# Gated cross-attention and a top-2 expert layer on one core: ranks behind scores and transposes, five groups for six, shares and values on GpSimd, block tables handed over in two parts

## The chip, the cores and the metric

One Trainium2 chip, one core. The metric is device time in microseconds (us) of one execution, median over the runs; lower is better. Engines: PE (TensorE, its weight loads PEld), DVE (VectorE), ACT (ScalarE), POOL (GpSimd), SP (SyncE, which only issues DMAs here). The engines run their own instruction streams and meet at semaphores.

## What is computed

Eight batches of 256 rows of 256 features. First a gated cross-attention over 120 context rows, then a gated mixture of 8 experts with the two best experts per row.

```
x = x + tanh(g_xattn) * attention(layernorm(x), ctx)      # 16 query heads summed to 4, rope, mean over heads, @ Wo
# ffn of layernorm(x), rows flattened to T = 2048:
probs = softmax(x @ gate_w.T);  w, idx = top_k(probs, 2);  w = w / w.sum()
for e in range(8):                                        # combine[t, e] = w where e was picked
    g, u = split(x @ gate_up[e].T, 2)                     # 1024 each
    acc += combine[:, e] * ((silu(g) * u) @ down[e].T)
x = x + tanh(g_ffn) * acc
```

## The kernel before, in words

The work has two halves. The first goes batch by batch through the attention and picks two experts for each row. The second is a loop over blocks: the 4096 picks are sorted by expert, each expert's list is cut into blocks of 128 rows, and PE runs each block through its expert.

First half. All engines run the same loop `for t in range(B + 1)`, a software pipeline: round t works on scores of batch t+1 (`scores`), transposes the probabilities of batch t (`transpose_probs`), mixes its values (`mix_values`), and finishes batch t-1 (`transpose_o`, `attend`; then on DVE `best_two`, which begins with two MAX8 on the gate logits, and `add_residual`, `normalise_o`). ACT does the exponentials and copies out of PSUM, POOL the reciprocal roots, and in the first rounds both split the first expert's weights into a high and a low part.

The routing is done for groups of batches, `SETS`. With `ENDS[b]` the group that ends with batch b: in round b+1 DVE makes the group's choice (`choose`: eight small steps that give `pick` and `chosen`) and `logit_gap`; in round b+2 PE counts, for each pick, how many came before it on its expert (`ranks`, small bf16 matmuls that need `chosen_ready`), DVE turns the ranks into slots (`ranks_of_picks`, `slots`, with a `value` that carries the token's number) and shares (`share_out`: the weight per expert, written beside the row in `x`), POOL marks with a compare against 0..127 at which place in its block each pick goes (`mark_places`, four per batch, called "hits" below), DVE marks which blocks begin at or before its slot, times the value (`mark_slots`, four per batch); in round b+3 PE multiplies the two (`invert`, four matmuls per batch, each two passes and so x8 in the trace), which writes each token's number at its slot, and DVE adds the result up (`add_places`). The marks live in a ring of `DEPTH` = 3 batches. SP stores a group's rows with shares and norm terms in DRAM (`store_rows`). At the end of the loop stand the last inversion, `find_tokens` (the list `token_at`), and the block tables on DVE: which expert each block has, how many blocks there are, where its index column lies (`bases_ready`), and at which block the pieces of the next expert's weights have to be split (`piece_at`, `piece_code`, then `tables_ready`). Meanwhile PE runs `stay_warm(10)`, matmuls whose result nobody reads.

Second half. POOL gathers the rows of each block (indirect DMA, four in flight) and scatters the results with an add. ACT applies the norm (`stage`), PE transposes the block (`transpose_x`), ACT and DVE split it into two fp32r parts (`x_high`, `x_low`), PE expands it in two halves (`expand`), ACT applies silu (`gate`), DVE multiplies (`product`), PE transposes (`transpose_h`) and contracts (`contract`). The next expert's weights are loaded and split beside it. Step 0 stands ahead of the loops; ACT and PE wait for `tables_ready` ahead of it.

## Time and profile before

| | |
|---|---|
| median of 3 runs | 470.66 us (469.97 to 474.62) |
| profiled execution | 469.98 us |
| its span | 468.2 us |
| mean granted TensorE clock | 0.958 |
| PE busy | 429.1 us, 92% |
| PEld / DVE / ACT / POOL busy | 357.5 / 223.0 / 199.2 / 253.7 us |

The span runs from the first to the last record of the profiler; what lies around it belongs to the execution's time too. Busy time of PE is modelled at its ends. A timeline row has start, length, engine, line, operation, output and inputs, the number of instructions merged in it, and in brackets the engine's idle time before it and what ended it. The number after L is the line in the kernel before.

### The profile page before, as it was taken

Reading aid. Unit: us, or ns where it says so; the run is one execution under the profiler, and the core shown is the slowest. Engines: PE = TensorE matmul, PEld = TensorE weight load, DVE = VectorE, ACT = ScalarE, POOL = GpSimd, SP = SyncE. Lnnn points to the kernel's source line nnn. Section 1 sums busy time; section 2 is a strip of 40 time slices with the busy share of each in tenths; the row PEclk is TensorE's granted clock in tenths of the full one; section 3 lists DMA queues with packets and bytes.
Section 4 is the critical chain, followed back from the end, with each engine's and each line's share of the span. In section 5 each row is a group of like instructions: output and inputs, shape, how many; then the busy total and the mean of one; then the engine's idle time right before and its main releaser. Section 6 shows DMA issues by size and latency. Waiting matters only on the chain.

```text
span 468.2 us, 10992 instructions
## 1 busy us (share of the span) xinstructions
PE 429.1 (92%) x2541; PEld 357.5 (76%) x2542; DVE 223.0 (48%) x625; ACT 199.2 (43%) x388; POOL 253.7 (54%) x255
## 2 busy tenths in 40 slices
PE   7899978885999999999999999999999999999960
PEld 6656555763478888888888888888888888888850
DVE  2465979656633434344434444444434443444330
ACT  2477644400166235634633743364336435523310
POOL 3119646433438634972992794269526954954321
PEclk9999999766999999999999999999999999999985
DMA  8950035612104512461353165116411642111211
GB/s 274 401 210 25 22 100 162 216 46 70 36 12 148 180 24 32 123 205 23 101 174 86 26 199 135 23 23 202 124 34 23 202 120 39 22 25 26 47 25 11
DMA packets 19579, 46.54 MB, mean 99 GB/s; under 512 B 2380, under 2 KB 13716, under 8 KB 16468
## 3 DMA queue, kind: packets, MB, share of 16 engines
q1 hardware_dynamic: 11648, 35.20, 22.1%
q0 software_dynamic: 6720, 9.64, 11.2%
q10 hardware_dynamic: 1188, 1.44, 0.9%
q8 instruction: 9, 0.15, 0.1%
q14 instruction: 14, 0.11, 0.1%
HBM read 37.54 MB, written 9.00 MB: 99 GB/s over the span
## 4 chain that ended last, share of the span: by engine, by line
PE 82%; DVE 8%; DMA 3%; issue 3%; ACT 2%; POOL 1%; POOLq 1%; SPq 0%; DVEq 0%
PE sc L908 20%; PE att L928 20%; PE misc L908 10%; PE qbank L908 10%; PE pT L918 6%; PE sc L734 2%; PE att L822 2%; DMA x<-in_x 2%; PE sc L752 2%; PE att L892 2%; PE att L791 2%; PE misc L776 1%; DVE dn L1121 1%; PE att L716 1%; PE misc L768 1%
## 5 line engine op out<-in xcount | busy, mean ns | idle before, releaser
L928 PE MATMUL att<-dn,hT 128*128 x816 | 115.0, 291 | 0.0
L463 POOL DMA_INDIRECT out<-xT_all,index_out x34 | 54.5, 1604 | 109.7 <-DVE xT_all L1315 101.3
L908 PE MATMUL sc<-gu,xT 128*128 x408 | 103.0, 401 | 0.0
L928 PEld LDWEIGHTS att<-dn,hT 128*128 128x128 f32 x816 | 102.7, 192 | 0.1
L908 PEld LDWEIGHTS sc<-gu,xT 128*128 128x128 f32 x408 | 74.2, 188 | 15.0
L908 PE MATMUL misc<-gu,xT 128*128 x204 | 80.0, 392 | 1.7 <-ACT xT L638 0.9
L908 PE MATMUL qbank<-gu,xT 128*128 x204 | 79.9, 392 | 0.0
L374 POOL TENSOR_TENSOR gu<-wraw,gu 128x2048 f32 x14 | 64.5, 4624 | 10.1 <-ACT gu L556 8.0
L1289 DVE TENSOR_TENSOR xT_all<-xT_all,sc 128x512 f32<-128x512 f32 x34 | 23.4, 687 | 88.3 <-ACT xT_all L645 88.3
L1289 DVE TENSOR_TENSOR xT_all<-xT_all,qbank 128x512 f32<-128x512 f32 x34 | 23.4, 688 | 64.1 <-ACT xT_all L645 64.1
L645 ACT ACTIVATE xT_all<-misc 128x512 f32<-128x512 f32 x34 | 20.3, 598 | 71.7 <-PE qbank L908 71.7
L1293 DVE TENSOR_TENSOR hT<-pT,hT 128x512 fp32r<-128x512 f32 x68 | 46.5, 684 | 2.8 <-issue 2.8
L908 PEld LDWEIGHTS misc<-gu,xT 128*128 128x128 f32 x204 | 38.4, 188 | 9.2 <-issue 2.3
L456 POOL DMA_INDIRECT xT_all<-rows_scratch,index_in x37 | 36.7, 993 | 14.2 <-issue 10.4
L908 PEld LDWEIGHTS qbank<-gu,xT 128*128 128x128 f32 x204 | 38.4, 188 | 7.1
L918 PE MATMUL pT<-const,xT_all 128*128 128x128 f32 x272 | 40.7, 272 | 2.0 <-issue 2.0
L918 PEld LDWEIGHTS pT<-const,xT_all 128*128 128x128 f32 x272 | 33.8, 140 | 10.9 <-issue 2.2
L649 ACT ACTIVATE hT<-pT 128x512 fp32r<-128x512 f32 x68 | 40.3, 592 | 3.5 <-PE pT L918 3.5
L645 ACT ACTIVATE xT_all<-sc 128x512 f32<-128x512 f32 x34 | 20.2, 593 | 47.4 <-PE sc L908 47.4
L556 ACT ACTIVATE gu<-wraw 128x2048 f32 (+1 forms) x16 | 30.7, 1920 | 11.4 <-PE att L928 7.5
L374 POOL TENSOR_TENSOR dn<-wraw,dn 128x2048 f32 x7 | 32.2, 4603 | 0.0
L389 POOL TENSOR_SCALAR vareps<-mv 128x2 f32<-128x2 f32 (+1 forms) x11 | 2.5, 231 | 53.3 <-DVE mv L996 53.2
(152 smaller groups left out, 529.7 us busy)
## 6 DMA issues: line engine op xcount, KB each, us to landing
wraw<-in_gu SPq DMA_DIRECT2D x16, 1024.0 KB, 5.5
wraw<-in_dn SPq DMA_DIRECT2D x8, 1024.0 KB, 5.1
x<-in_x SPq DMA_DIRECT2D x8, 266.0 KB, 11.3
xT_all<-in_xT SPq DMA_DIRECT2D x4, 512.0 KB, 11.3
out<-x SPq DMA_DIRECT2D x8, 256.0 KB, 2.2
rows_scratch<-x SPq DMA_DIRECT2D x2, 532.0 KB, 5.4
rows_scratch<-x SPq DMA_DIRECT2D x4, 266.0 KB, 2.7
xT_all<-rows_scratch,index_in POOLq DMA_INDIRECT x37, 2.9
```

Of the source, the lines that this page charges most:

```text
L374: nc.gpsimd.tensor_tensor(piece_of(where, 1, p), wraw[:, p * PIECE:(p + 1) * PIECE], piece_of(where, 0, p), ALU.subtract).then_inc(w_lo, 1)
L456: nc.gpsimd.indirect_dma_start(out=xg[:, q, :], out_offset=None, in_=rows_d, in_offset=bass.IndirectOffsetOnAxis(ap=index, axis=0)) .then_ ...
L463: nc.gpsimd.indirect_dma_start(out=out_d, out_offset=bass.IndirectOffsetOnAxis(ap=index, axis=0), in_=y[:, r, :], in_offset=None, compute_ ...
L556: nc.scalar.activation(piece_of(where, 0, p), wraw[:, p * PIECE:(p + 1) * PIECE], ACT.Copy).then_inc(w_hi, 1)
L645: nc.scalar.activation(silu[:, hf, :], bank[2 * hf][:, :], ACT.Silu).then_inc(silu_made, 1)
L649: nc.scalar.activation(hT[:, hf, 0, :], bank[4 + hf][:, :], ACT.Copy).then_inc(hT_hi, 1)
L734: nc.tensor.matmul(sc[:, 1, :], ident, const[:, 0:512], start=True, stop=True)
L908: mm = nc.tensor.matmul(bank[2 * hf + n][:, :], xT[:, par, xp, k, :], gu_part(where, wp, k * 2 * I + col, HALF), start=(k == 0 and xp == 0 ...
L918: mm = nc.tensor.transpose(bank[4 + hf][:, j * P:(j + 1) * P], h[:, hf, j * P:(j + 1) * P], ident)
L928: mm = nc.tensor.matmul(bank[6][:, 0:D], hT[:, hf, hp, j * P:(j + 1) * P], dn_part(where, wp, (hf * JH + j) * D, D), start=(hf == 0 and j ...
L1289: V.tensor_tensor(h[:, hf, :], silu[:, hf, :], bank[2 * hf + 1][:, :], ALU.mult).then_inc(h_made, 1)
L1293: V.tensor_tensor(hT[:, hf, 1, :], bank[4 + hf][:, :], hT[:, hf, 0, :], ALU.subtract)\
```

## The change

Five groups instead of six: batches 4 and 5 form one. The ring of marks is four deep; the fourth place of the hits and the running sum lie in another buffer that is free by then. On PE the ranks come behind the second scores, in the last round behind the transposes of batch 7, and batches 4 and 5 are inverted behind the last round. The shares and the values are made by POOL, the value is multiplied into the hits there, and DVE's block marks become one wide compare per batch. The last batch's hits are split, two on POOL and two on DVE. In the last round the choice is put in front of the second moments. On DVE the tables up to the block ends are made ahead of the last sum; the tables are handed over in two parts: PE waits for `experts_ready` alone, and the low part of block 0 (`x_low(0, 0)`) is made between the two parts. POOL gathers block 1 ahead of the other index copies. The filler is four matmuls instead of ten.

```diff
-SETS = ((0, 1), (2, 3), (4,), (5,), (6,), (7,))
+SETS = ((0, 1), (2, 3), (4, 5), (6,), (7,))
-DEPTH = 3
+DEPTH = 4
+BY_POOL = 2
...
+            def share_out(g):
+                a, z = tiles_of(g)
+                n = z - a
+                pool.wait_ge(chosen_ready, g + 1)
+                pool.wait_ge(odds_ready, g + 1)
+                n_step[0] += 1
+                nc.gpsimd.tensor_tensor(wpart[:, 0:n, :, :], pick[:, a:z, :, :],
+                                        odds[:, a:z, :].rearrange("p t (k o) -> p t k o", o=1).broadcast_to([P, n, 2, E]),
+                                        ALU.mult).then_inc(pool_step, 1)
+                pool.wait_ge(pool_step, n_step[0])
+                nc.gpsimd.tensor_tensor(x[:, a:z, D:D + E], wpart[:, 0:n, 0, :], wpart[:, 0:n, 1, :], ALU.add)\
+                  .then_inc(row_ready, 1)
+            def place_values(g):
+                a, z = tiles_of(g)
                 pool.wait_ge(slot_ready, g + 1)
+                nc.gpsimd.tensor_tensor(
+                    value[:, a:z, :], c("token")[:, a:z].rearrange("p (t o) -> p t o", o=1).broadcast_to([P, z - a, 2]),
+                    place[:, a:z, :], ALU.subtract).then_inc(value_ready, 1)
+                pool.wait_ge(value_ready, g + 1)
...
-                    ins = nc.gpsimd.tensor_scalar(at_place[:, b % DEPTH, i, :], c("place"), place[:, t, k:k + 1], None,
-                                                  ALU.is_equal)
+                    ins = nc.gpsimd.tensor_scalar(at_place[b % DEPTH][:, i, :], c("place"), place[:, t, k:k + 1],
+                                                  value[:, t, k:k + 1], ALU.is_equal, ALU.mult)
...
-            mark_places(B - 1)
+            share_out(NS - 1)
+            place_values(NS - 1)
+            mark_places(B - 1, BY_POOL)
...
-            for s in range(1, RING):
+            keep_index(index_in, 1, 1)
+            pool.wait_ge(index_kept, 1)
+            gather(1, 1, index_in[:, 1:2])
+            for s in range(2, RING):
                 keep_index(index_in, s, s)
...
             pe.wait_ge(x2_ready, B)
-            invert(B - 2, B - 2, B - 1)
+            late = SETS[NS - 3][0]
+            for b in SETS[NS - 3]:
+                invert(b, late, B - 1)
             ranks(NS - 1)
-            invert(B - 1, B - 2, B - 1)
+            invert(B - 2, late, B - 1)
+            invert(B - 1, late, B - 1)
...
-            stay_warm(10)
+            stay_warm(4)
             transpose_x(0)
-            pe.wait_ge(tables_ready, 1)
+            pe.wait_ge(experts_ready, 1)
...
-                for i in range(PICKS):
-                    t, k = TB * b + i // 2, i % 2
-                    ins = V.tensor_scalar(upto[:, b % DEPTH, i, :], c("begin"), slot[:, t, k:k + 1], value[:, t, k:k + 1],
-                                          ALU.is_le, ALU.mult)
-                ins.then_inc(upto_ready, 1)
+                V.tensor_tensor(upto[:, b % DEPTH, :, :],
+                                c("begin").rearrange("p (o n) -> p o n", o=1).broadcast_to([P, PICKS, SLOTS + 1]),
+                                slot[:, TB * b:TB * (b + 1), :].rearrange("p t (k o) -> p (t k) o", o=1)
+                                .broadcast_to([P, PICKS, SLOTS + 1]), ALU.is_le).then_inc(upto_ready, 1)
...
-            link(V.tensor_scalar(last_block[:, :], endblk[:, E - 1:E], -1.0, None, ALU.add))
+            V.tensor_scalar(last_block[:, :], endblk[:, E - 1:E], -1.0, None, ALU.add).then_inc(experts_ready, 1)
+            x_low(0, 0)
```

PE, from the transposes of batch 7 in the last round to the first of block 0. First before; `misc<-xT_all,gc` are those transposes, L804 to L814 the ranks, L822 the inversion, L791 attending, L734 the filler.

```order
L814 MATMUL sc<-chosen,before_bf 128x16
L776 MATMUL misc<-xT_all,gc 8x256 x2
L779 MATMUL misc<-const,on 64x128 x2
L822 MATMUL att<-dn 128x137 x4
L791 MATMUL att<-wo,oT 128x264 x2
L822 MATMUL att<-dn 128x137 x4
L804 MATMUL sc<-base_bf,ones_bf 128x24
L806 MATMUL sc<-chosen,ones_bf 128x24 x14
L812 MATMUL sc<-chosen,ones_bf 128x16
L812 MATMUL sc<-chosen,ones_bf 128x8
L814 MATMUL sc<-chosen,before_bf 128x24
L822 MATMUL att<-dn 128x137 x4
```

And the same place in the changed kernel, where L840 to L850 are the ranks, L860 the inversion and L827 attending.

```order
L815 MATMUL misc<-const,on 64x128 x2
L840 MATMUL sc<-base_bf,ones_bf 128x16
L842 MATMUL sc<-chosen,ones_bf 128x16 x12
L848 MATMUL sc<-chosen,ones_bf 128x8
L850 MATMUL sc<-chosen,before_bf 128x16
L827 MATMUL att<-wo,oT 128x264 x2
L860 MATMUL att<-dn 128x137 x8
L840 MATMUL sc<-base_bf,ones_bf 128x24
L842 MATMUL sc<-chosen,ones_bf 128x24 x14
L848 MATMUL sc<-chosen,ones_bf 128x16
L848 MATMUL sc<-chosen,ones_bf 128x8
L850 MATMUL sc<-chosen,before_bf 128x24
```

Behind it follow the inversions of batches 6 and 7 (x4 and x4) and four fillers. The ranks have moved behind the transposes, no inversion stands ahead of attending, and eight matmuls of inversion stand ahead of the last ranks where four stood.

DVE, from the last marks to the end of the tables. Before, L1121 are the block marks, L1142 and L1145 the shares, L1130 and L1134 the last sum and the token list.

```order
L1121 TENSOR_SCALAR dn<-const,slot_f,value 128x137 x4
L1233 COPY ends_f<-sc 128x8
L1236 TENSOR_TENSOR area<-ends_f,const 128x128
L1238 TENSOR_REDUCE nblk<-area 128x8
L1142 TENSOR_TENSOR route<-route,odds 128x32
L1145 TENSOR_TENSOR x<-route 128x2x8
L1130 TENSOR_TENSOR dn<-att,dn 128x137
L1134 SCALAR_TENSOR_TENSOR token_at<-dn,const 128x136
L1242 TENSOR_TENSOR area<-const,nblk 128x64
```

In the changed kernel L1172 and L1176 are the last sum and the list, L1181 is `x_low(0, 0)`, and the piece tables begin at L1296.

```order
L1281 MEMSET skip 128x1
L1172 TENSOR_TENSOR area<-att,area 128x137
L1176 SCALAR_TENSOR_TENSOR token_at<-area,const 128x136
L1283 TENSOR_TENSOR area<-endblk,const 128x352
...
L1291 TENSOR_SCALAR tab<-tabf 128x44
L1292 TENSOR_SCALAR last_block<-endblk 128x1
L1181 TENSOR_TENSOR xT<-att,xT 128x256
L1296 COPY piece_at<-startblk 128x8
L1297 TENSOR_SCALAR piece_at<-nblk 128x8
```

The block ends stand ahead of the last sum now, the shares are gone from DVE, and `x_low(0, 0)`, which waits for ACT, stands between the two parts of the tables; before it was behind them.

## Rows read from the trace of the kernel before

**Rows 1.** Busy time by window; the columns are named in the prediction.

```profile
86.50:97.00 10.50, 8.75 (x57) 6.96 (x57) 6.03 (x31) 1.94 (x5) 3.72 (x8) 0.67 0.49 152
97.00:106.00 9.00, 6.35 (x35) 4.14 (x35) 6.00 (x31) 0.75 (x3) 3.71 (x8) 0.62 0.17 59
...
133.90:468.20 334.30, 318.50 (x1942) 281.14 (x1942) 137.39 (x304) 143.67 (x253) 195.59 (x158) 0.98 0.32 84
```

**Rows 2.** Timeline, 52 to 64 us: POOL's split and hits, a cast, first inversion.

```profile
52.57 5.03 POOL L380 TENSOR_TENSOR dn<-wraw,dn 128x512 fp32r<-128x512 f32 x4
52.60 1.27 DVE L1107 CAST slot_f<-slot_i 128x16 f32<-128x16 int32 x1
...
57.81 4.67 POOL L419 TENSOR_SCALAR dn<-const,slot_f 128x128 f32<-128x128 f32 x8 [0.21 <-POOL dn L380]
...
62.82 2.04 PE L822 MATMUL att<-dn 128*128 128x137 f32 x16
```

**Rows 3.** Timeline, 66 to 106 us: the rounds' marks and the round to 76.40.

```profile
66.69 0.25 DVE L1047 MAX8 top<-att 128x8 f32<-128x8 f32 x2 [2.14 <-PE att L791]
...
70.06 0.23 PE L812 MATMUL sc<-chosen,ones_bf 128*128 128x24 bf16 x3 [1.16 <-DVE chosen L1075]
...
71.33 1.16 DVE L1027 TENSOR_REDUCE negmax<-sc 128x8 f32<-128x960 f32 x1 [0.26 <-DVE route L1095]
...
73.43 4.67 POOL L419 TENSOR_SCALAR dn<-const,slot_f 128x128 f32<-128x128 f32 x8 [0.27 <-DVE slot_f L1107]
...
74.07 2.81 ACT L566 ACTIVATE gu<-sc,shift,rs 128x120 f32<-128x120 f32 x8
74.09 2.39 DVE L1121 TENSOR_SCALAR dn<-const,slot_f,value 128x137 f32<-128x137 f32 x8
...
76.40 0.23 DVE L1047 MAX8 top<-att 128x8 f32<-128x8 f32 x2
...
85.86 0.25 DVE L1047 MAX8 top<-att 128x8 f32<-128x8 f32 x2 [1.68 <-PE att L791]
...
96.46 0.25 DVE L1047 MAX8 top<-att 128x8 f32<-128x8 f32 x2 [2.28 <-PE att L791]
...
105.55 0.25 DVE L1047 MAX8 top<-att 128x8 f32<-128x8 f32 x2 [0.80 <-PE att L791]
```

**Rows 4.** Timeline, 107 to 115 us: the last group's ranks, marks and inversion.

```profile
107.08 1.21 PE L822 MATMUL att<-dn 128*128 128x137 f32 x8 [1.57 <-DVE x L1080]
...
109.71 0.19 DVE L1095 TENSOR_TENSOR route<-route,sc 128x32 f32<-128x32 f32 x1 [0.35 <-PE sc L814]
...
110.63 2.42 POOL L419 TENSOR_SCALAR dn<-const,slot_f 128x128 f32<-128x128 f32 x4 [0.86 <-DVE slot_f L1107]
110.69 1.31 DVE L1121 TENSOR_SCALAR dn<-const,slot_f,value 128x137 f32<-128x137 f32 x4
...
113.10 2.20 PE L822 MATMUL att<-dn 128*128 128x137 f32 x8 [3.43 <-POOL dn L419]
```

**Rows 5.** Timeline, 115 to 134 us: filler, tables, step 0, the loop's first matmul.

```profile
115.09 10.53 PE L734 MATMUL sc<-const 128*128 128x512 f32 x20
...
116.99 0.57 DVE L1250 TENSOR_TENSOR area<-endblk,const 128x352 f32<-128x352 f32 x1
...
120.01 0.60 ACT L631 ACTIVATE xT_all<-xT_all 128x256 f32<-128x256 f32 x1 [10.28 <-DMA xT_all<-rows_scratch,token_at]
...
120.34 0.15 DVE L1259 TENSOR_SCALAR last_block<-endblk 128x1 int32<-128x1 f32 x1
...
125.16 0.21 DVE L1277 TENSOR_TENSOR tab<-tabf 128x44 int32<-128x44 f32 x1
...
126.74 0.49 PE L908 MATMUL misc<-gu,xT 128*128 x1 [0.91 <-ACT xT L638]
...
129.84 1.28 ACT L645 ACT_TABLE_LOAD   x1 [2.43 <-PE qbank L908]
...
133.90 0.49 PE L908 MATMUL misc<-gu,xT 128*128 x1 [0.71 <-issue]
```

More of the change, by code:

```diff
@@ L190, in build_program @@
         hits = dn[:, 1, :, :].rearrange("p q n -> p (q n)").bitcast(F32)
-        at_place = hits[:, 0:DEPTH * PICKS * P].rearrange("p (q i n) -> p q i n", q=DEPTH, i=PICKS)
-        at = DEPTH * PICKS * P
-        upto = hits[:, at:at + DEPTH * PICKS * (SLOTS + 1)].rearrange("p (q i n) -> p q i n", q=DEPTH, i=PICKS)
-        at += DEPTH * PICKS * (SLOTS + 1)
-        from_begin = hits[:, at:at + SLOTS + 1]
-        assert at + SLOTS + 1 <= 2 * DN
+        at = DEPTH * PICKS * (SLOTS + 1)
+        upto = hits[:, 0:at].rearrange("p (q i n) -> p q i n", q=DEPTH, i=PICKS)
+        places = [hits[:, at + q * PICKS * P:at + (q + 1) * PICKS * P] for q in range(DEPTH - 1)]
+        assert at + (DEPTH - 1) * PICKS * P <= 2 * DN
+        at = E * NT + 2 * NCOL * E
+        places.append(area[:, at:at + PICKS * P])
+        at_place = [ap.rearrange("p (i n) -> p i n", i=PICKS) for ap in places]
+        at += 2 * NCOL * E
+        from_begin = area[:, at:at + SLOTS + 1]
+        assert at + SLOTS + 1 <= KC * B * A and PICKS * P <= 2 * NCOL * E
         late = xT_all[:, :, :].rearrange("p k n -> p (k n)")
@@ L430, in _ @@
                     score_scale(t + 2, 2)
-                for b in range(B):
-                    if SETS[SET_OF[b]][-1] + 2 == t:
-                        mark_places(b)
+                if t - 2 in ENDS:
+                    share_out(ENDS[t - 2])
+                    place_values(ENDS[t - 2])
+                    for b in SETS[ENDS[t - 2]]:
+                        mark_places(b, PICKS)
                 if t - 1 in ENDS:
@@ L855, in _ @@
                     transpose_probs(t, 0)
-                if t - 2 in ENDS:
-                    ranks(ENDS[t - 2])
                 if t + 1 < B:
                     scores(t + 1, 1)
+                if t < B and t - 2 in ENDS:
+                    ranks(ENDS[t - 2])
                 if t >= 1:
                     transpose_o(t - 1)
+                if t == B:
+                    ranks(NS - 2)
                 if t < B:
```

67 lines of the change are left out of this document (28 added, 39 removed).

## The prediction, as it was put on record

> **What bounds the kernel now.** I read the table of windows first [rows 1]. Its columns are start:end, length, busy time and instruction count of PE, weight loads, DVE, ACT and POOL, granted clock, DMA share, GB/s. From 133.9 us on PE is busy 318.5 of 334.3 us: this is the loop over the experts' blocks, bound by TensorE, and its code stays as it is. So whatever is won ahead of the loop should come out at the end one for one, and I only follow the date of the loop body's first matmul, 133.90 [rows 5]. Ahead of it, in 86.5 to 106, PE is busy 15.1 of 19.5 us at a granted clock of 0.67 and 0.62, between its levels of 1.2 and 2.4 GHz: no engine is full there, it is a chain that goes round DVE, PE, ACT and POOL. I then read the timeline of each round. The rounds are marked by DVE's first look at a batch's attended rows (MAX8), at 66.69, 76.40, 85.86, 96.46 and 105.55 [rows 3]. The end of that chain is in [rows 4, 5].
>
> **Round by round.** G is how much earlier the changed kernel gets to a mark.
>
> Up to 66.69. DVE loses the shares and gets 2 wide compares for 8 narrow marks, and would be over a microsecond earlier. But the inversion of batches 0 and 1 waits for POOL's eight hits, which fill 57.81 to 62.48, right behind its weight split, and the inversion runs at 62.82 [rows 2]. POOL now makes shares and values ahead of them, three small operations. The trace has none of them on POOL; they lie between 0 and three times a hit (0.58, on more columns), and I take 0.9 with their waits. Hits are then ready at 63.4. PE reaches them early, has batch 0 done by then, and ends 0.5 before its time now. G = 0.5.
>
> To 76.40 the round is bound by DVE: 8 marks take 2.39 us from 74.09, and MAX8 follows directly [rows 3]. A compare of 548 columns isn't in the trace: 352 columns take 0.57 (116.99 [rows 5]), in proportion that is 0.89; floor 0.57, ceiling the four marks that it replaces, 1.2. I take 0.75, both 1.5, which saves 0.9 (0 to 1.25). Shares and value go to POOL, 0.45. The second scores stand ahead of the ranks, which takes away the 0.26 idle at 71.33. Sum 1.6: G = 2.1, if PE's side is as early, and it is: its transposes no longer stand behind the second scores.
>
> To 85.86: before, batch 4 was a group, and its choice and ranks stood in a row ahead of the transposes. They are gone from here. What is late next are the exponentials, from 74.07 on, 2.81 us [rows 3], only 0.75 earlier than now: done at 76.1. Second scores to 76.95, transposes 1.35, probabilities 0.45: 78.75. The hits of batch 3 are there at about 78.7, since POOL starts its marks at 74.0 after shares (now 73.43, 4.67 for eight). Inversion 1.9, attending and mixing 1.8, hop 0.2: 82.6. G = 3.3.
>
> To 96.46, 10.6 us now. The choice of a four-tile group takes 3.4 us from MAX8 to the ranks' release (66.69 to 70.06 [rows 3]), the ranks 0.2: 86.2. Transposes 2.4 at 1.2 GHz, probabilities 0.85, no inversion behind them (about 2), 2.1 to MAX8: 91.6. At 2.4 GHz the same three are 1.4, 0.45, 1.8: 89.9. G = 4.9 or 6.6.
>
> To 105.55, 9.1 us now. The transposes of batch 7 no longer wait for a choice: residual and normalise 1.6, transposes 2.4, ranks 0.7, then DVE's slots 1.0 and a wide compare 0.75: 6.4 us at 1.2 GHz, 5.4 at 2.4. MAX8 at 98.0 or 95.3. G = 7.5 or 10.2. POOL makes the hits of batches 4 and 5 from 90.3 to 95.0, in time.
>
> **The tail**, from MAX8 at 105.55 to the end of the last inversion at 115.30, takes 9.75. Moving the choice ahead of the moments takes 1.0 off the choice, but buys nothing: PE now has two batches to invert first. A batch's four matmuls (x8 in the rows) ran in 1.21 at 2.4 GHz (107.08) and in 2.20 at 1.2 (113.10) [rows 4], 0.94 and 1.85 where they follow each other. Two batches start 1.5 behind MAX8, end 3.4 or 5.2 behind it, and the ranks come out 4.1 or 6.2 behind it, against 4.1 now (109.71). This is where the price of one group less falls due. Slots 0.85, POOL's value 0.3, two hits on each of POOL and DVE 1.2 (instead of 2.42 on POOL), inversion 2.2: 10.8 at 1.2 GHz. At 2.4 GHz POOL's own queue is last (norm, shares, hits), some 9.9. The inversion ends at 98.0 + 10.8 = 108.8, or 95.3 + 9.9 = 105.2. G = 6.5 or 10.1. A granted clock of 0.62 to 0.67 [rows 1] is two thirds of the time low, so I take two thirds of the one and one third of the other: 7.7.
>
> **From the inversion to the loop**, 115.30 to 133.90, 18.6 us now. PE's filler (20 passes, 10.53 us [rows 5]) lasts until 125.6, while the row block is staged from 120.01 on. With four filler matmuls, 8 passes: five at 0.86 before the clock rises, three at 0.43, 5.6 us, against 5.3 for the block. So transposes at +5.7, ACT's copy to +6.5, expand at +6.9 (now +11.4). experts_ready is in time: DVE comes out of the inversion with the block ends made, adds 0.75, and by_block to last_block (116.99 to 120.49) takes 3.5: +4.25. That gives 4.5. But DVE now waits for ACT's copy before the piece tables, which take 4.84 (120.53 to 125.37 [rows 5]) and are done at +11.8. ACT's silu waits for tables_ready, and a table load of 1.28 goes ahead of it (129.84). Load, silu 0.6, product 0.7, transposes 0.6, loop entry 0.7, hops: the loop's first matmul at +15.9, against +18.6. So of 4.5 us at the first matmul 2.7 are left at the loop; PE stands about 1.9 in between. Row block 1 is no bound: its index is copied at +4.4, it lands at +8.
>
> Sum: 7.7 + 2.7 = 10.4. The profiled execution took 469.98 (its span 468.2 and 1.8 around it): 459.6 for it. The median of the runs shown is 0.7 above, so 460.3 us.
>
> **A rule weighed.** The rows show POOL's four hits in 2.42 (110.63) beside DVE's marks in 1.31, and eight in 4.67 (73.43) with DVE's marks beside half of them: 0.6 each, no wait. But at 52.60 a cast of 16 columns took 1.27 beside POOL's two-input split, where such small operations take 0.15 to 0.21 (120.34, 125.16) [rows 2 to 5]. So a lock exists, and the hits don't meet it.
> The Trainium skill, page SBUF — State Buffer, section Who interferes with whom, says that a DVE instruction with two SBUF inputs contends with a GpSimd instruction that reads SBUF, and that the one that comes later blocks for the whole of the other. By that rule the first rival is the one to expect. By the rows it isn't: under the same section the old marks should have blocked too.
>
> **Rivals.**
> - The lock. The wide compares have two inputs, the old marks one. If each compare waits for one hit (0.6), at the four places where it is on the path, that is 2.4: 462.7. Chance 0.15.
> - The clock stays down. PE gets gaps of 1.2 us behind the filler and 1.9 behind step 0's expansion, and only 5.6 us of filler instead of 10.5. If the clock doesn't come back in it, the filler takes 1.3 more, and step 0 ends 4.4 later (each half 2.85 more, part of it in the gap). With the low clock all through that is 6.5 + 2.7 - 5.7 = 3.5: 467.2. For it: clock 0.62 and 0.67 in the stretches with gaps. Against: the filler has none. Chance 0.10.
> - The gain is hidden: POOL's queue or ACT's exponentials bind the middle rounds, G stops at 4: 4 + 2.7, 464.0. For it: both end within 0.5 us of PE's need in my own sums. Chance 0.13.
> - Slower: a hit with a second operation (compare, then multiply by the value) costs more on POOL. The trace has it only without. Nearest rows: 0.58, and 1.26 for a two-input operation of four times the columns (52.57, four in 5.03). At 1.24 eight hits take 9.9: batches 0 and 1 at 68.7, 2 and 3 at 89.2, 4 and 5 at 109.8, 7 at 122.5, end of the inversion 124.7, 9.4 late, less 2.7: 477.4. It decides from about 1.0 us a hit on. I take 0.58: the columns are the same. Chance 0.05.
> - The forecast itself, within 457 to 462: 0.57.
>
> **Numbers.** A measurement of this kernel can tell about 1% (4.7 us). Forecast, lock and hidden gain lie below 465.95, the low clock above it. Faster 0.86, same 0.09, slower 0.05. The range goes from every round at 2.4 GHz (10.1 + 2.7: 457.9, and 1 for small errors) to the low clock: 457 to 467.
>
> **What would show it.** Right: MAX8 of batches 4 to 7 near 74, 83, 91, 97; two inversions between the last residual and the last ranks; 8 passes of filler; silu's first table load behind tables_ready; PE idle between step 0's expansion and its transposes; the loop as long as before. Wrong: POOL's hits over 0.7 us each; wide compares over 0.9; a granted clock of 0.5 in the first block; PE waiting inside the loop, on split weights above all.

## The result, and the profile after

The changed kernel took 466.9 us, median of 4 runs (466.20 to 468.91), against 471.23 for the kernel before (4 runs, 469.97 to 474.62): ratio 0.9891, 95% interval 0.9845 to 0.9937. The same program launched again (`after_again`, below) took 470.05 (12 runs, 467.02 to 474.32): ratio 0.9951, interval 0.9921 to 0.9981. It is faster by 0.5 to 1.1%, 2 to 4 us; the forecast was 10.4 us less. Medians here are over all executions, the ratios leave out the few that took over 1.5% more than the fastest of the same kernel. The profiled execution took 466.59, its span 464.8, mean granted clock 0.944 (before: 0.958).

The windows that answer to [rows 1], with the last one from the new date of the loop's first matmul on:

```profile
86.50:97.00 10.50, 8.58 (x51) 6.57 (x51) 6.02 (x25) 2.64 (x9) 4.38 (x9) 0.61 0.38 125
...
97.00:106.00 9.00, 7.11 (x35) 4.32 (x33) 6.55 (x29) 0.86 (x3) 7.92 (x15) 0.50 0.27 91
...
130.20:464.80 334.60, 319.36 (x1942) 281.53 (x1942) 137.60 (x304) 144.01 (x254) 195.65 (x158) 0.97 0.33 84
```

The loop is as long as before (334.6 for 334.3), so its first matmul decides, as forecast: 130.19 for 133.90. In the second row POOL is busy 7.92 of 9.00 us, where it had 3.71, and the clock is at its lower level throughout. Round 4 and the marks of the rounds, from the timeline (answers to [rows 2, 3]):

```profile
55.71 1.19 DVE L1147 CAST slot_f<-slot_i 128x16 f32<-128x16 int32 x1
...
58.02 1.44 DVE L1153 TENSOR_TENSOR dn<-const,slot_f 128x548 f32<-128x548 f32 x2
58.33 0.54 POOL L426 TENSOR_TENSOR route<-route,odds 128x64 f32<-128x64 f32 x1 [0.24 <-POOL dn L388]
...
59.83 6.26 POOL L448 TENSOR_SCALAR dn<-const,slot_f,value 128x128 f32<-128x128 f32 x8
...
64.64 1.11 PE L860 MATMUL att<-dn 128*128 128x137 f32 x8
...
66.15 1.21 PE L860 MATMUL att<-dn 128*128 128x137 f32 x8 [0.40 <-POOL dn L448]
...
69.18 0.25 DVE L1090 MAX8 top<-att 128x8 f32<-128x8 f32 x2 [3.42 <-PE att L827]
...
77.19 0.23 DVE L1090 MAX8 top<-att 128x8 f32<-128x8 f32 x2
...
87.27 0.25 DVE L1090 MAX8 top<-att 128x8 f32<-128x8 f32 x2 [4.17 <-PE att L827]
...
97.67 0.25 DVE L1090 MAX8 top<-att 128x8 f32<-128x8 f32 x2 [3.94 <-PE att L827]
...
104.85 0.25 DVE L1090 MAX8 top<-att 128x8 f32<-128x8 f32 x2 [0.63 <-PE att L827]
```

Eight hits with their multiply take 6.26, 0.78 each; without it they took 4.67 [rows 3]. The mark of batch 3 is 2.5 us later than before, not 0.5 earlier. Only the smaller part of that is the hits: the inversion waits 0.40 us for those of batch 1, but PE itself reached batch 0's inversion at 64.64, 1.8 us later than before (62.82 [rows 2]), with its hits already made. The last mark is 0.7 earlier, for 7.5 or 10.2 forecast. The tail, from the chain of waits that ended last (start, length, what):

```profile
105.39 3.17 POOL dn L448 x4
...
108.95 0.74 POOL x L399
...
111.12 0.76 POOL value L437
...
111.98 1.68 POOL area L448 x2
...
113.70 1.22 PE att L860 x8
```

It is mostly one queue, POOL's: hits of batch 6, norm, shares and value, two hits of batch 7. PE and DVE come out together with it: the value waits 0.18 us for DVE's slots, which need PE's last ranks. The transition, from the timeline (answers to [rows 5]):

```profile
114.74 3.60 PE L770 MATMUL sc<-const 128*128 128x512 f32 x8
...
119.81 0.60 ACT L667 ACTIVATE xT_all<-xT_all 128x256 f32<-128x256 f32 x1 [9.55 <-DMA xT_all<-rows_scratch,token_at]
...
121.67 0.49 PE L951 MATMUL misc<-gu,xT 128*128 x1 [0.77 <-ACT xT L674]
...
130.19 0.50 PE L951 MATMUL misc<-gu,xT 128*128 x1 [0.53 <-issue]
```

From the end of the last inversion (114.91) to the loop it is 15.3 us for 18.6.

### The profile page after: what moved, and what is told of

It is laid out like the page before. It is cut to its first block, busy times and chain, and to the rows that moved or that the text cites. A ratio compares the mean times of both kernels' runs of the same rounds, so it can differ in the third digit from the quotient of the medians.

```text
span 464.8 us, 10899 instructions
## 1 busy us (share of the span) xinstructions
PE 431.6 (93%) x2518; PEld 359.0 (77%) x2519; DVE 215.8 (46%) x571; ACT 199.9 (43%) x388; POOL 263.3 (57%) x264
## 3 DMA queue, kind: packets, MB, share of 16 engines
q10 hardware_dynamic: 1188, 1.44, 0.9%
## 4 chain that ended last, share of the span: by engine, by line
PE 79%; POOL 6%; DVE 4%; DMA 3%; issue 3%; ACT 2%; POOLq 1%; SPq 0%; DVEq 0%; ACTq 0%
PE sc L951 20%; PE att L971 20%; PE misc L951 10%; PE qbank L951 10%; PE pT L961 6%; POOL dn L448 2%; DMA x<-in_x 2%; PE sc L788 2%; PE att L935 2%; PE misc L804 2%; PE att L827 1%; PE att L752 1%; POOL dn L388 1%; PE att L860 1%; PE misc L812 1%
## 5 line engine op out<-in xcount | busy, mean ns | idle before, releaser
L382 POOL TENSOR_TENSOR gu<-wraw,gu 128x2048 f32 x14 | 64.5, 4618 | 10.2 <-ACT gu L592 8.2
L489 POOL DMA_INDIRECT xT_all<-rows_scratch,index_in x37 | 36.7, 992 | 13.1 <-issue 10.7
L961 PEld LDWEIGHTS pT<-const,xT_all 128*128 128x128 f32 x272 | 33.8, 140 | 10.8 <-issue 2.2
L397 POOL TENSOR_SCALAR vareps<-mv 128x4 f32<-128x4 f32 (+1 forms) x10 | 2.3, 234 | 43.7 <-DVE mv L1039 43.4
```

Source lines behind the costliest of these rows:

```text
L382: nc.gpsimd.tensor_tensor(piece_of(where, 1, p), wraw[:, p * PIECE:(p + 1) * PIECE], piece_of(where, 0, p), ALU.subtract).then_inc(w_lo, 1)
L489: nc.gpsimd.indirect_dma_start(out=xg[:, q, :], out_offset=None, in_=rows_d, in_offset=bass.IndirectOffsetOnAxis(ap=index, axis=0)) .then_ ...
L961: mm = nc.tensor.transpose(bank[4 + hf][:, j * P:(j + 1) * P], h[:, hf, j * P:(j + 1) * P], ident)
```

## The experiments

Each kernel was profiled once and timed in 4 to 12 runs beside the kernel before, whose medians in the five sets were 472.09, 471.80, 472.17, 471.86 and 470.85. The marks, in us of the profiled span: MAX8 of batches 2, 5 and 7, end of the last inversion, the loop's first matmul; then the median.

| kernel | b2 | b5 | b7 | inverted | loop | median |
|---|---|---|---|---|---|---|
| before | 59.62 | 85.86 | 105.55 | 115.30 | 133.90 | 471.2 |
| changed | 59.38 | 87.27 | 104.85 | 114.91 | 130.19 | 466.9 |
| after_again | 58.42 | 93.66 | 110.52 | 120.62 | 134.97 | 470.1 |
| trans_only | 59.71 | 87.57 | 105.38 | 115.13 | 129.44 | 465.9 |
| trans_busy | 62.81 | 89.05 | 104.41 | 113.13 | 129.31 | 467.0 |
| value_moved | 61.38 | 90.82 | 108.42 | 119.60 | 138.20 | 474.2 |
| values_back | 60.74 | 85.34 | 100.57 | 110.20 | 127.02 | 465.5 |
| ranks_first | 61.16 | 90.87 | 108.45 | 119.82 | 135.26 | 469.9 |
| six_groups | 58.95 | 86.99 | 104.35 | 115.05 | 130.56 | 469.1 |
| keep_busy | 57.93 | 93.16 | 106.26 | 119.66 | 134.04 | 470.3 |
| cover_wait | 56.97 | 87.75 | 100.85 | 114.36 | 128.74 | 468.4 |
| narrow_marks | 63.37 | 90.06 | 103.39 | 117.66 | 132.17 | 466.3 |
| values_busy | 60.10 | 84.69 | 98.49 | 107.17 | 121.59 | 458.3 |

**trans_only: the transition alone.** The kernel before with these lines of the change and nothing else:

```diff
-            stay_warm(10)
+            stay_warm(4)
...
-            pe.wait_ge(tables_ready, 1)
+            pe.wait_ge(experts_ready, 1)
```

with the new order of the tables, `x_low(0, 0)` between their parts, and block 1's gather first.

> The kernel before with the part behind the last inversion alone: block ends ahead of the last sum, tables in two parts with the low part of block 0 between them, block 1's gather first, four fillers for ten. Rounds, groups, marks and shares as before. Theory A (the measured gain is the transition's alone, the rounds gave nothing): end of the last inversion at 115.3 as before, the loop's first matmul at 130.5 to 131.0 instead of 133.9, 466.5 to 467.3 us for a profiled 470.0, so as fast as the changed kernel. Theory B (the rounds gained and the clock took it back in the transition): only 2.7 us or less of it shows here, 467.3 to 468.5.

465.85 us, ratio 0.9867 (0.9823 to 0.9911). Theory A: the last inversion ends where it did, and the measured gain of the whole change is the transition's. This part alone is as fast as the change. It gave more than forecast, since the table load was not behind the tables:

```profile
124.91 1.28 ACT L648 ACT_TABLE_LOAD   x1 [1.02 <-PE qbank L911]
...
126.44 0.20 DVE L1286 TENSOR_TENSOR tab<-tabf 128x44 int32<-128x44 f32 x1
...
129.44 0.49 PE L911 MATMUL misc<-gu,xT 128*128 x1 [0.73 <-DVE xT_all L1293]
```

The load (1.28) runs ahead of the end of the tables (126.64), hidden behind DVE, and the loop begins 14.3 behind the inversion, for 15.9 forecast.

**values_back: shorter hits.** The changed kernel with

```diff
-                                                  value[:, t, k:k + 1], ALU.is_equal, ALU.mult)
+                                                  None, ALU.is_equal)
```

in POOL's hits, and the value back in DVE's four narrow marks per batch.

> The changed kernel with the value back in DVE's block marks (four narrow marks per batch) and POOL's hits a compare alone. Theory POOL (the hit with its second operation, 0.78 us for 0.58, holds the rounds): eight hits take 4.7 instead of 6.3, the first inversion at 64.5 instead of 66.15, MAX8 of batch 3 at 68 instead of 69.2, of batch 7 near 103, 1.5 us or more off the whole. Theory clock (from 88 us on PE at 1.2 GHz is the bound, and the hits are covered): the early marks come forward by up to 1 us, MAX8 of batch 7 stays within 0.7 of 104.9, the time within 1 us of the changed kernel's.

465.52 (0.9813 to 0.9929), 1.4 under the changed kernel and 4.5 under its second launch; the interval overlaps that of the first (0.9845 to 0.9937). Hits 4.66 for eight. The first inversion no longer waits, but PE comes to it at 64.97, and MAX8 of batch 3 is at 68.84 for 69.18: in round 4 shorter hits gain little. MAX8 of batch 7 is at 100.57, the end of the inversion 4.7 earlier, of which 1.5 is lost again up to the loop. The marks speak for theory POOL, the time does not decide it.

**ranks_first: the order.**

```diff
+                if t < B and t - 2 in ENDS:
+                    ranks(ENDS[t - 2])
                 if t + 1 < B:
                     scores(t + 1, 1)
-                if t < B and t - 2 in ENDS:
-                    ranks(ENDS[t - 2])
```

> The changed kernel with the ranks ahead of the second scores again (rounds 3, 5 and 7). Theory order (the ranks behind the scores put the small slot steps of the first group beside POOL's weight split): ranks near 49.9 instead of 51.5, the slot steps at 0.2 us each instead of 1.1, the projection at 57.37 about 1.5 earlier, MAX8 of batch 3 near 67.5 instead of 69.2. If that is what the rounds lost, batch 7 comes 1.5 earlier too (103.3) and the whole 1.5 less. Theory clock: what is won by 69 us is gone by 98, since PE at 1.2 GHz takes the rounds over; the time within 1 us of the changed kernel's.

469.87 (0.9927 to 0.9975), not better; its profile had another stretch of low clock before round 3 (38 to 45 us), in code that is the same, so its marks can't be compared one by one. In time the order gains nothing.

**keep_busy: PE's clock.** Unread matmuls where PE waits, `idle(n)` being n of the first line:

```diff
+                    nc.tensor.matmul(qbank[:, 0:240], ident, const[:, 0:240], start=True, stop=True)
...
+                    if t == 7:
+                        idle(4)
                     ranks(ENDS[t - 2])
+                if t == B:
+                    idle(2)
...
+            idle(2)
             pe.wait_ge(x2_ready, B)
...
             invert(B - 2, late, B - 1)
+            idle(5)
             invert(B - 1, late, B - 1)
...
-            stay_warm(4)
+            stay_warm(6)
             transpose_x(0)
+            stay_warm(1)
```

> The changed kernel with matmuls whose result nobody reads where PE waits: four of 240 columns ahead of the ranks in round 7, two ahead of the transposes and two ahead of the first inversion in the last round, five between the inversions of batches 6 and 7; six fillers for four and one behind block 0's transposes. Theory clock: the granted clock stays at 1.0 from 90 to 109 us, the same work is done about 4 us sooner (MAX8 of batch 7 near 101.5, end of the last inversion near 111), step 0's first expansion takes 3.4 instead of 4.4, the whole 4 to 5 us less, 462. Rival (POOL and DVE hold the rounds, PE's clock is not what sets them): the clock is up, and the marks move less than 1 us. Rival (the clock falls whatever PE does there): clock 0.5 as before, and the added matmuls cost 1 to 3 us.

470.25 (0.9871 to 0.9958), where 462 was forecast: no better as a whole. The windows tell why (columns as in [rows 1]):

```profile
66.00:80.00 14.00, 12.18 (x48) 9.27 (x49) 4.51 (x21) 0.60 (x1) 4.55 (x9) 0.51 0.29 95
...
96.00:112.00 16.00, 12.35 (x111) 9.18 (x107) 13.20 (x58) 2.58 (x9) 13.26 (x24) 1.00 0.46 157
```

And PE's timeline:

```profile
64.76 1.18 PE L865 MATMUL att<-dn 128*128 128x137 f32 x8 [2.79 <-issue]
...
67.82 2.19 PE L865 MATMUL att<-dn 128*128 128x137 f32 x8 [1.88 <-POOL dn L448]
...
113.97 2.19 PE L865 MATMUL att<-dn 128*128 128x137 f32 x8 [3.93 <-POOL dn L448]
```

Where the matmuls stand the clock holds, and MAX8 of batch 5 to MAX8 of batch 7 takes 13.1 for 17.6, 4.5 us less, as theory clock said. But the tail grows from 10.1 to 13.4, waiting for POOL's hits, and in code that was left alone PE stood still for 2.79 and 1.88 us in round 4, and the clock was down from 66 on. Both are waits for hits, the first too: batch 0's four end at 64.66.

**after_again: the same program.**

> The changed kernel once more, nothing edited. keep_busy was the same program up to round 7, and yet TensorE's granted clock fell at other places in it (38 to 41 and 65 to 78 us) than in the changed kernel's profile (48, 59, 79, 89 to 109 us). Theory W (where the clock falls differs from one launch to the next, how much of it falls is the kernel's): MAX8 of batch 3 and the places of the low stretches are others than before, by up to 4 us, the time 466 to 469 as before. Theory S (the places belong to the program): the same marks within 0.6 us as in the changed kernel's profile.

470.05, above the 466 to 469 that both theories gave. Theory W for the rest: MAX8 of batch 3 at 74.00 for 69.18. The timeline of round 4 in this launch:

```profile
54.94 5.92 POOL L388 TENSOR_TENSOR dn<-wraw,dn 128x512 fp32r<-128x512 f32 x4
55.99 2.52 DVE L1153 TENSOR_TENSOR dn<-const,slot_f 128x548 f32<-128x548 f32 x2
...
61.99 6.25 POOL L448 TENSOR_SCALAR dn<-const,slot_f,value 128x128 f32<-128x128 f32 x8
...
68.30 2.19 PE L860 MATMUL att<-dn 128*128 128x137 f32 x8 [1.88 <-POOL dn L448]
```

```profile
66.00:80.00 14.00, 12.12 (x50) 9.31 (x49) 4.06 (x19) 2.14 (x6) 4.78 (x7) 0.54 0.27 88
```

That fence is the timeline, this one the window behind it. Here DVE's wide compares fell beside POOL's weight split: 2.52 for 1.44, and the split 5.92 for 4.94 (in the changed kernel's first profile they began as the split ended, 58.02). The hits came 2.2 later: the split began 1.8 later and took 1.0 more, and the shares behind it took 0.6 less. PE waited, and the clock was at its lower level for most of the next 14 us. The single rows, from narrower windows of the same timeline, tell who held whom:

```profile
55.99 0.80 DVE L1153 TENSOR_TENSOR dn<-const,slot_f 128x548 f32<-128x548 f32 x1
...
56.17 1.75 POOL L388 TENSOR_TENSOR dn<-wraw,dn 128x512 fp32r<-128x512 f32 x1
...
56.71 1.79 DVE L1153 TENSOR_TENSOR dn<-const,slot_f 128x548 f32<-128x548 f32 x1
...
57.88 1.75 POOL L388 TENSOR_TENSOR dn<-wraw,dn 128x512 fp32r<-128x512 f32 x1
```

Alone a piece of the split takes 1.26 and a compare 0.72. The second compare (1.79) ends 0.6 behind the piece that was running when it began, and the next piece (1.75) ends 1.13 behind that compare: each comes out as if it had waited for the other to end.

**values_busy: both.** values_back and keep_busy in one kernel.

> values_back and keep_busy in one: hits without the second operation, value in DVE's block marks, and unread matmuls in PE's waits from round 7 on. In keep_busy the clock held from 80 to 112 us and the stretch from MAX8 of batch 5 to MAX8 of batch 7 took 13.1 instead of 17.6, but then the inversion of batch 6 waited 3.9 for POOL's hits and the tail to the inversion's end took 13.4 instead of 10.1. Theory two covers (with the clock up POOL's hits at 0.78 are the next bound; with it down PE hides them): here the hits cost 0.58, the last stretch takes 13 and the tail at most 10.5, so the end of the last inversion lies 3 us or more ahead of both, and the time is 461 to 463. Theory clock alone: as keep_busy, the tail over 12, time 465 or more. Rival: the unread matmuls themselves lengthen the tail; then the tail is over 12 here too though the hits are ready.

458.26 (456.59 to 459.74, 6 runs), ratio 0.9719 (0.9683 to 0.9755), better than the 461 to 463 forecast; launched again beside narrow_marks 458.52 (0.9685 to 0.9757). Theory two covers. Timeline and windows:

```profile
92.33 4.68 POOL L444 TENSOR_SCALAR dn<-const,slot_f 128x128 f32<-128x128 f32 x8
...
99.68 2.15 PE L861 MATMUL att<-dn 128*128 128x137 f32 x16 [1.82 <-DVE x L1128]
...
102.12 1.19 PE L861 MATMUL att<-dn 128*128 128x137 f32 x8
...
105.96 1.21 PE L861 MATMUL att<-dn,area 128*128 128x137 f32 x8 [0.63 <-POOL area L444]
```

```profile
80.00:96.00 16.00, 15.54 (x124) 12.45 (x124) 11.25 (x51) 6.40 (x18) 6.57 (x14) 1.00 0.69 213
96.00:112.00 16.00, 13.54 (x80) 9.61 (x80) 13.26 (x59) 0.97 (x5) 9.97 (x22) 1.00 0.24 80
```

The wait of 3.93 for batch 6's hits is gone, the last is 0.63, the clock is 1.00. Alone the two edits gave 1.4 to 4.5 us and nothing; together 8.6 against the changed kernel's first launch, 11.8 against its second.

**trans_busy: PE's clock in the old rounds.** trans_only with unread matmuls in rounds 7, 8 and the tail.

> trans_only with unread matmuls of 240 columns in PE's waits of the last two rounds and the tail (four ahead of the ranks in rounds 7 and 8, three ahead of the first late inversion, one ahead of the last ranks, seven ahead of the last inversion). Theory clock (in the old rounds too the low clock costs): clock 1.0 from 90 to 118 instead of half of it at 0.5, end of the last inversion 2 us earlier than trans_only's 114.9, filler 3.6 instead of 5.3 without an effect, 463.5 to 464.5 us. Rival (the old rounds are a chain through DVE, PE's clock is beside the point): the clock is up and the inversion's end within 0.7 us of trans_only's.

467.01 (0.9882 to 0.9952), for 463.5 to 464.5 forecast and trans_only's 465.85. The last rounds are shorter (b5 to b7 15.4 for 17.8), but batch 2 was 3.1 late in this launch, and from the inversion to the loop it took 16.2 for 14.3. Inconclusive on the whole; no gain.

**six_groups** and **vb_six_groups:** batches 4 and 5 apart again, in the changed kernel and in values_busy.

```diff
-SETS = ((0, 1), (2, 3), (4, 5), (6,), (7,))
+SETS = ((0, 1), (2, 3), (4,), (5,), (6,), (7,))
```

> The changed kernel with batches 4 and 5 as groups of their own again, the ring still four deep. Theory merge (one group less takes a choice and ranks out of the rounds, and is worth 1 us or more): round of batch 6 waits for ranks of batch 4 again, MAX8 of batch 7 later by 1 to 2 us, the tail from MAX8 to the inversion's end shorter by about 1.5 (one batch to invert less), so 0 to 1 us slower in all. Rival (the merge only moved the inversions behind the last round, where they are on the path): as fast or 1 us faster than the changed kernel.

469.12 (0.9897 to 0.9971): as the changed kernel's second launch, within 1 us. MAX8 of batch 7 was to come 1 to 2 us later and came 0.5 earlier; the tail is 10.7 for 10.1. The rival.

> values_busy with batches 4 and 5 as groups of their own. six_groups lay within 1 us of the changed kernel at a low clock. Theory merge (with PE at full clock the rounds are a chain, and a choice and its ranks more in it cost): MAX8 of batch 7 at 99.5 to 101 for 98.5, of which the tail gives back 1 us (its first inversion is one batch): 459 to 460. Rival: no difference above 0.5 us, 458.3, the merge was worth nothing. Rival: the tail gives back more than the rounds lose, 457.5.

461.14, 2.9 over values_busy and over all three forecasts, but the intervals overlap (0.9686 to 0.9776 for 0.9683 to 0.9755). b5 to b7 takes 14.1 for 13.8 and the tail 8.7 for 8.7. So the merge was worth 0.3 us in the marks, where my sums for the last two rounds rested on it.

**vb_ranks_first:** values_busy with the ranks ahead of the second scores.

> values_busy with the ranks ahead of the second scores in rounds 3, 5 (in round 7 there are no second scores). Theory order (in round 3 the late ranks set the slot steps beside POOL's split, each 1.1 for 0.2): MAX8 of batch 2 near 59, of batch 3 near 67 for 68.2, and 1 us of it kept to the end: 457.3. Rival (the wait for the choice comes back ahead of the scores, 0.9 and 1.2 us in the kernel before): MAX8 of batch 4 later than 77.2, the time 458.3 to 459.5.

459.71 (0.9686 to 0.9780). Its profile is the only one without a low stretch before the loop, 456.22 in that run. Not separable from values_busy.

**vb_filler_only:** values_busy without the unread matmuls in the rounds and the tail.

> values_busy without the unread matmuls in the rounds and the tail, with the seven fillers around block 0's transposes alone. values_back took 465.5, values_busy 458.3: this splits the 7.3 us between the rounds and the transition. Theory rounds (the clock in rounds 7 and 8 and the tail is what they buy): MAX8 of batch 7 near 100.6 to 101 and the last inversion's end near 110 as in values_back, against 98.5 and 107.2; only the step 0 part (9.6 instead of 10.0 to 10.7 us from its first matmul to the loop) comes back, 463 to 465. Theory transition (the fillers are what counts): 459 to 461.

461.96 (0.9725 to 0.9818), between the two forecasts, 3.7 over values_busy with intervals that touch (up to 0.9755 there). The marks speak for theory rounds: b5 to b7 takes 15.3 for 13.8, the tail 10.2 for 8.7, and the clock is 0.50 from 98 to 106.

**vb_shares_dve:** values_busy with the shares on DVE.

> values_busy with the shares back on DVE, as the kernel before has them. Theory helps (POOL's queue is short of time, DVE's too, shares cost each about the same): in the last round POOL's hits start 0.6 to 0.9 us earlier, DVE's marks 0.45 later, MAX8 of batches 3 and 4 0.4 later, the time within 1 us of values_busy's 458.3. Theory DVE binds the rounds (as I forecast, 0.45 per group): 1 to 1.5 us slower, 459.5.

465.46 (0.9798 to 0.9896), 7.2 us slower, the intervals apart: both theories missed it. DVE's timeline in round 7, and PE's behind it:

```profile
91.62 0.23 DVE L1187 TENSOR_TENSOR route<-route,odds 128x64 f32<-128x64 f32 x1 [1.64 <-ACT odds L618]
```

```profile
95.86 1.87 PE L797 MATMUL misc<-xT_all,gc 128*8 128x256 f32 x4 [1.70 <-DVE on L1074]
```

DVE waits 1.64 for ACT's odds in front of its marks, PE then waits 1.70 for DVE, and the clock falls (0.5 from 96 to 104). In values_busy, which has the shares on POOL, DVE has no such wait. So this part of the change, which I had booked at 0.45, is worth several us there, the clock behind it included.

**value_moved: the longer hits and the wide compare**, in the kernel before:

```diff
-                    ins = nc.gpsimd.tensor_scalar(at_place[:, b % DEPTH, i, :], c("place"), place[:, t, k:k + 1], None,
-                                                  ALU.is_equal)
+                    ins = nc.gpsimd.tensor_scalar(at_place[:, b % DEPTH, i, :], c("place"), place[:, t, k:k + 1],
+                                                  value[:, t, k:k + 1], ALU.is_equal, ALU.mult)
```

> The kernel before with one edit: the value is multiplied into POOL's hits, DVE's block marks are one wide compare per batch. Groups, order, shares, tables as before. Theory hits (POOL's eight hits at 0.78 make PE wait in round 4, and TensorE's clock falls behind that wait): eight hits take 6.3, the inversion of batch 1 waits 1.5 us or more for them, a low stretch begins within 3 us of it that the kernel before did not show (there the clock was 1.00 from 10 to 86 us), MAX8 of batch 3 is 1.6 to 5 us later than 66.7, and the time is 1 to 4 us over the kernel before: 473 to 476. Rival (DVE's 0.9 us saved per two batches pays for the hits): the time within 1 us of the kernel before, 471 to 473. Rival (faster, DVE bound those rounds): 470 or less.

474.18 (12 runs), ratio 1.0050 (1.0031 to 1.0070): slower by 0.3 to 0.7%. Timeline and window:

```profile
58.98 2.48 DVE L1120 TENSOR_TENSOR dn<-const,slot_f 128x548 f32<-128x548 f32 x2
...
67.54 1.21 PE L823 MATMUL att<-dn 128*128 128x137 f32 x8 [1.86 <-POOL dn L420]
```

```profile
66.00:80.00 14.00, 12.43 (x64) 8.87 (x64) 7.15 (x32) 4.34 (x15) 5.12 (x9) 0.76 0.30 95
```

The wait is there, and behind it a low stretch (70 to 77) that the kernel before did not have. MAX8 of batch 3 is at 71.08 for 66.69, but 1.8 of that was lost before batch 2; from there it takes 9.7 for 7.1. Theory hits, with two reservations: eight hits took 6.98 here, the first 1.55 beside the second compare, so the multiply and the wide compare are not told apart; and a wait alone doesn't bring the clock down. In the kernel before, PE waited longer in that round, and the clock stayed up:

```profile
61.17 1.03 PE L776 MATMUL misc<-xT_all,gc 128*8 128x256 f32 x4 [2.01 <-DVE on L1039]
```

```profile
60.00:87.00 27.00, 22.72 (x165) 17.45 (x166) 21.48 (x88) 13.15 (x38) 13.90 (x27) 1.00 0.47 148
```

**cover_wait: PE's wait filled.** keep_busy with eight more unread matmuls:

```diff
+                        if t == 4:
+                            for _ in range(5 if b == 0 else 3):
+                                nc.tensor.matmul(att[:, 1, 0:240], ident, const[:, 0:240], start=True, stop=True)
                         invert(b, group[0], group[-1])
```

> keep_busy (hits at 0.78, unread matmuls from round 7 on) with unread matmuls of 240 columns in round 4 as well: five ahead of batch 0's inversion, three ahead of batch 1's, where PE waited 1.1 to 2.8 and 1.9 us for POOL's hits in after_again and keep_busy and the clock was 0.5 from 67 to 80. Theory wait (the low stretch follows from PE's wait): no low stretch between 65 and 80, MAX8 of batch 3 13 us or less behind MAX8 of batch 2 (15.6 in both those runs), the upper half of keep_busy's times (470 to 473) gone: a median of 465 to 468. Rival (the clock falls there whatever PE does): low stretch as before, 15.6 or more, a median of 470 to 472.

468.43 (463.90 to 472.57), ratio 0.9898 (0.9859 to 0.9937). The inversion still waits 0.67, and the window reads

```profile
66.00:80.00 14.00, 12.64 (x78) 9.15 (x78) 9.56 (x37) 5.04 (x15) 6.83 (x14) 0.93 0.30 99
```

with 1.00 up to 78 us; MAX8 of batch 2 to 3 takes 12.9 for 15.6. Theory wait, for this stretch of this one profile. It is of an execution of 465.13, and keep_busy had such executions too (465.17, 465.22); in time the two kernels can't be told apart, and the upper times did not go away. In the tail (13.5) POOL holds here too.

**narrow_marks: hit or compare.** keep_busy with narrow compares for the wide one. values_busy differs in where the value is made and multiplied in: on DVE, where here POOL makes it and multiplies it into the hits.

```diff
+                for i in range(PICKS):
+                    t, k = TB * b + i // 2, i % 2
+                    ins = V.tensor_scalar(upto[:, b % DEPTH, i, :], c("begin"), slot[:, t, k:k + 1], None, ALU.is_le)
+                ins.then_inc(upto_ready, 1)
```

> keep_busy with DVE's block marks as four narrow compares per batch (no value) for the one wide compare; the hits on POOL stay with their second operation at 0.78. values_busy differs from this in the hits alone, keep_busy in the wide compare alone. Theory hit (the 0.2 us of the second operation is what holds the rounds): PE waits 0.4 us or more for POOL's hits in round 4, the tail from MAX8 of batch 7 to the inversion's end 11.5 or more, the time 465 to 470, near keep_busy's 470.3. Theory lock (a wide compare with two inputs beside POOL's split made the split 5.9 for 4.9 and itself 1.26 for 0.72, and that made the hits late): POOL's split takes 4.9 to 5.0 here in every case, no wait of PE over 1 us for the hits of batches 0 and 1, the time 459 to 462, near values_busy's. Both about half: 462 to 466.

466.31 (463.14 to 469.75), ratio 0.9890 (0.9854 to 0.9927). The split took 4.94, but the marks began only as it ended, so this profile doesn't show them side by side; values_busy_2 does, below. PE did not wait in round 4, against theory hit, but late in the tail it does:

```profile
110.49 2.19 PE L865 MATMUL att<-dn 128*128 128x137 f32 x8 [3.19 <-POOL dn L448]
```

So the value on POOL, with its multiply in the hits, costs 7.8 us here (466.3 to 458.5, the intervals apart). Some 1.7 of it is my own doing: behind the low clock the unread matmuls in the tail ended that much after the last hits. The wide compare's part is not settled: the medians differ by 3.9 (470.3 to 466.3), the ratios by 0.25%, 1.2 us, with intervals that overlap (0.9871 to 0.9958 for keep_busy).

**values_busy_2:** values_busy launched again.

> values_busy once more, nothing edited, beside narrow_marks on the same chip. 457.5 to 460.5; low stretches before 65 us at other places than before, none behind 66.

458.52. The clock was low from 11 to 15 and from 62 to 66 us, and not behind that, as forecast.

## Why the prediction was wrong, point by point

**Direction and end of the chain: right.** The time went where I looked, ahead of the loop, and the loop stayed as long. 466.9 lies just inside the range of 457 to 467, but 6.6 above the 460.3 forecast, and the second launch (470.05) lies outside. By stretches, in us:

| stretch | before | forecast | changed | values_busy |
|---|---|---|---|---|
| to MAX8 of batch 3 | 66.69 | 66.2 | 69.18 | 68.19 |
| batch 3 to 4 | 9.71 | 8.1 | 8.01 | 9.05 |
| batch 4 to 5 | 9.46 | 8.3 | 10.08 | 7.45 |
| batch 5 to 6 | 10.60 | 9.0 or 7.3 | 10.40 | 7.50 |
| batch 6 to 7 | 9.09 | 6.4 or 5.4 | 7.18 | 6.30 |
| batch 7 to the inversion's end | 9.75 | 10.8 or 9.9 | 10.06 | 8.68 |
| from there to the loop | 18.60 | 15.9 | 15.28 | 14.42 |

**The transition: right, undersized.** 2.7 forecast; 3.3 in the changed kernel, 4.3 in trans_only. The term that failed is the table load behind `tables_ready`: the load doesn't wait for the tables, and in trans_only it is hidden. In the changed kernel's first profile the clock fell within step 0's first expansion (0.50 at 124 to 126), the load came behind it at 126.13, and 1 us of the gain went back.

**The rounds: 7.7 forecast, 0.4 measured.** 3.0 of the 7.3 are lost by batch 3, the rest between batches 4 and 7. Four steps failed.
- "PE reaches them early, has batch 0 done by then." It didn't. The last ranks of the first group ran at 51.5, not at 49.5 as before: the second scores now stand ahead of them, and the clock was at its lower level from 48 to 51. Three small steps of DVE then fell beside POOL's split and took 1.14, 1.07 and 1.19, where before one of them did (the cast, 1.27), and the query projection behind them ran at the lower clock (0.57 over 58 to 62). So PE came to the inversion 1.8 late, without a wait for hits. Shares and value on POOL, booked at 0.9, took 1.7 from the split's end (58.09) to the first hit, as the shares ran beside the wide compares.
- "I take 0.58: the columns are the same." A hit with its multiply takes 0.78. I let it decide only from 1.0 on, since I weighed its own microseconds: 0.2 times 8 is 1.6. By the marks of batch 3 (values_back 0.3 earlier) it costs little there; it tells in the tail, where POOL's queue is the chain, and most where the other waits are filled: value_moved, values_back alone and narrow_marks against values_busy go the same way, and the last is clear of noise.
- "A lock exists, and the hits don't meet it." They do when a wide compare starts just ahead of one. In keep_busy and, in the kernel before, where a mark met the split:

```profile
105.59 0.75 DVE L1165 TENSOR_TENSOR dn<-const,slot_f 128x548 f32<-128x548 f32 x1
...
105.69 1.32 POOL L448 TENSOR_SCALAR dn<-const,slot_f,value 128x128 f32<-128x128 f32 x1
```

```profile
56.34 1.26 POOL L380 TENSOR_TENSOR dn<-wraw,dn 128x512 fp32r<-128x512 f32 x1
...
56.35 1.34 DVE L1121 TENSOR_SCALAR dn<-const,slot_f,value 128x137 f32<-128x137 f32 x1
```

The hit takes 1.32 for 0.79, the old mark 1.34 for 0.34 to 0.42, so the old marks did block, beside the split though not beside the hits. The wide compare also meets the split (2.52 for 1.44, and 5.92 for 4.94, in after_again), the shares (0.54 and 0.62 for 0.30 and 0.25) and the value (0.75 for 0.20). I had priced the rival for the compares alone, at 0.6 each. The Trainium skill, page SBUF — State Buffer, section Who interferes with whom, spoke for this contention, and I set it aside. The single rows of after_again agree with it: the operation that comes later ends as late as if it had waited for the other to end.
- "A granted clock of 0.62 to 0.67 is two thirds of the time low", taken over as a constant. The clock is an outcome. In the changed kernel it was 0.52 over 88 to 109 us, with POOL busy 15.1 of 21.0. With waits filled and short hits it is 1.00, and MAX8 of batch 5 to the end of the last inversion takes 22.5 us in values_busy, for 82.6 to 105.2, 22.6, forecast at 2.4 GHz. That the sums agree so well is in part luck: the two rounds took 1.1 more than forecast, the tail 1.2 less. What lies ahead of batch 5 was forecast 3.3 early and came 1.2 early even there.

**The rivals.** The hidden gain (POOL binds the middle rounds, 0.13) named the engine, the lock a mechanism that is there in more places than I gave it, and "the clock stays down" the right symptom, which I placed in the transition; it sat in the rounds. In values_busy against its one-sided variants they make each other worse, where I had given each a case of its own.

**What stays open.** Where the clock first falls differs between launches of one program: at 48 us in the changed kernel's profile, with PE busy 3.97 of the 4 us before, at 40 in after_again; near 48 in values_busy, at 11 and then at 62 in values_busy_2. Later marks differ by 1 to 5 us with it, and no run here explains it. Nor is it settled when a wait of PE brings the clock down: it fell behind 1.86 us in value_moved and not behind 2.01 in the kernel before. How the 7.3 us divide between clock, lock and hits in the changed kernel itself is not shown, since only taking the value off POOL and filling PE's waits together gave a gain over it that is clear of noise. Marks of two launches are best compared as differences within a launch.

## What to carry to other kernels

Price an operation that goes onto another engine at the queue it joins and beside what runs there, not at its own time: POOL had room on average (253.7 us of 468), and was the chain of the tail once hits, shares and values stood in a row. Look at single rows for contention, since merged ones hide who waited for whom. Take the clock as part of the result: filling TensorE's waits gave nothing by itself, shorter hits 1.4 to 4.5 us, both together 8.6 to 11.8. And measure the parts of a large change apart: here the transition alone was as fast as the whole change.

## What the runs showed of the hardware that I had not expected

- POOL's compare of 128 columns against a per-row value takes 0.58 us, with a multiply by a second per-row value 0.78.
- A two-input compare of 548 columns on DVE takes 0.72 us, and 1.79 where it began within a piece of POOL's split; the next piece then took 1.75 for 1.26 (after_again). Beside POOL's small shares the compare kept its time (0.70 and 0.82), and the shares took 0.54 and 0.62 for 0.30 and 0.25.
- Eight one-input marks of 137 columns took 2.39 beside POOL's hits and 5.37 beside the split (values_busy_2), which then kept its 4.94: there DVE alone pays.
- The same program, launched twice, had low clock at other places, and 3 us between its medians (466.9 and 470.05), more than the half-width of either interval.
